# A graph kernel on one core: VectorE's comparisons read their row of numbers from PSUM instead of SBUF

## Chip, cores and metric

One NeuronCore of a Trainium2 chip. The metric is the device time of one execution in microseconds (us). The runs of the kernel before gave 4217.88, 4217.89 and 4220.7 us, median 4217.89.

## What is computed

A graph of 3125 nodes with 128 features each and 103125 edges (source, destination, one of nine types). Three relational layers, a residual with a layer norm, then one attention layer with another residual and layer norm. Cut to what matters:

```python
for l in range(3):                                  # relational layers
    X = einsum('ne,ref->rnf', out, weights[l])      # x of each node by each type
    msg = X[edge_type, src] + biases[l][edge_type]
    out = segment_sum(msg, dest); out = relu(out) if l < 2 else out
x = layernorm(x + out)
# attention over the edges: alpha = beta * cosine(x[row], x[col]), softmax over each row's edges
x = layernorm(x + segment_sum(alpha[:, None] * x[col], row))
```

The attention is done on dense score blocks; for that the kernel needs, for each pair of nodes, how many edges join them. These counts don't depend on the layers, and they are made while the layers run.

## The kernel before, in words

The edges are first sorted by the node that sums them up, into 840 tiles of 128 edges (NT), in 31 groups of 102 nodes (MB, RB). Each of the three layers then goes through the 840 tiles, in 35 turns of 24 tiles (TURNS, BODY). For each tile of a layer:

- GpSimd gathers the 128 message rows of the edges with an indirect DMA (L925, 806 of them in a layer; some of the 840 tiles share a gather). It writes them into a ring of 62 slots (`grow`) and runs ahead of the rest: before gather t it waits until tile t - 30 was used (L922 to L924).
- SP counts the gathers that have landed (`pass_on`, L824 to L827) on a semaphore that TensorE waits for (L1043).
- VectorE makes a one-hot matrix of the tile (`one_hot`, L526): 102 numbers 0 to 101 compared with each edge's row, one row of `iota_w`, 32 bits wide, in SBUF. It works eight tiles ahead (U).
- TensorE multiplies one-hot and gathered rows into PSUM bank 6 or 7, four tiles to a bank in turn (L1046, two records a tile), and VectorE adds each product to the sums in SBUF (L596). TensorE's next four tiles wait for the additions of the group before last (L1045).

The counts of edges go on beside it, five cells to twelve tiles, in layers 0 and 1 and 14 turns of layer 2 (84 turns of 10 cells). A cell is 128 edges. VectorE makes two matrices of it with comparisons of a row of 16-bit numbers, `iota_h` in SBUF (`cell_hots`, L531 with 640 elements and L532 with 510), four cells ahead. TensorE multiplies them into the five banks 0 to 4, 128 x 510 each (L1057). When a group of 102 nodes is complete, 31 times in all, ScalarE copies the five banks out (L1206) and refills them (`refill`, L1188 to L1197), and TensorE waits for it (L1056).

The order on each engine is written out by hand. VectorE's order for a tile is: wait for the four tiles' product (L586), one-hot for eight tiles later, at five of twelve tiles also the two comparisons of a cell, then the addition (`take_tiles`, L579 to L596). TensorE's order is in `use_tiles` (L1035 to L1060); at the first cell of twelve tiles it loads five numbers into registers (L1054).

Between two layers the sums are transposed (`turn_sums`, L1062, `take_turned`, L598) and multiplied by the weights of the nine types (L1080, banks 5 to 7), VectorE adds the biases (L615), and SP writes the result to memory for the gathers, for which GpSimd waits.

Bank 5 is not used while the tiles of a layer go through. L724, in the attention stage, reads PSUM and a column of scalars; L556 is an integer operation of the preparation.

Of the kernel before, what the change touches and what calls it, by code (L numbers as in the profile page):

```python
# [20 lines left out]
BF16 = mybir.dt.bfloat16  # L21
F16 = mybir.dt.float16
# [6 lines left out]
P = 128  # L29
# [16 lines left out]
def gnn_program(nc, x, src, dst, edge_type, weights, biases, beta, out):  # L46
# [92 lines left out]
    with ExitStack() as ctx:  # L139
        def sb(name, shape, dt=F32):  # L140
            return ctx.enter_context(nc.sbuf_tensor(name, shape, dt))

        def sem(name):
            return ctx.enter_context(nc.semaphore(name))
# [8 lines left out]
        diag = sb("diag", [P, 3 * P], BF16)  # L153
        zerob = sb("zerob", [P, 512], BF16)
        ones = sb("ones", [P, P])
        iota_w = sb("iota_w", [P, CG * P])
        iota_h = sb("iota_h", [P, CG * P], F16)
        x0st = sb("x0st", [P, X0 - 2, 3 * D])
        arrays = sb("arrays", [P, 9, KW])
        gix, b7, tab = (arrays[:, n, :].bitcast(I32) for n in (0, 2, 3))  # L160
# [76 lines left out]
        ps = ctx.enter_context(nc.psum_tensor("ps", [P, 8, 512], F32))  # L237


        s_edges = sem("s_edges")  # L240
        s_const = sem("s_const")
        s_pool = sem("s_pool")
# [22 lines left out]
        s_wt = sem("s_wt")  # L265
        s_wc = sem("s_wc")
        s_pt = sem("s_pt")
        s_oh = sem("s_oh")
        s_used = sem("s_used")
        s_add = sem("s_add")  # L270
# [56 lines left out]
        def _(dve):  # L327
            steps = [0]

            def step(ins, mark=None):  # L330

                steps[0] += 1
                ins.then_inc(s_d, 1)
                dve.wait_ge(s_d, steps[0])
                if mark:
                    marks[mark] = steps[0]
# [185 lines left out]
                                               op0=ALU.mult, op1=ALU.add)  # L522
            step(ins, "digits")

            def one_hot(t):
                ins = nc_.tensor_scalar(oh[:, t % U, 0:RB], iota_r, rowf[:, t % NT:t % NT + 1], None, ALU.is_equal)  # L526
                if t % SLOTS == SLOTS - 1:
                    ins.then_inc(s_oh, 1)

            def cell_hots(q):  # L530
                nc_.tensor_scalar(cl[:, q % CR, :], iota_h[:, :], key1[:, q:q + 1], None, ALU.is_equal)  # L531
                nc_.tensor_scalar(cr[:, q % CR, :], iota_h[:, 0:CW], key2[:, q:q + 1], None, ALU.is_equal).then_inc(s_co, 1)  # L532


            dve.wait_ge(s_srt, 16)
# [8 lines left out]
            dve.wait_ge(s_pt, 1)  # L544
            nc_.tensor_scalar(gix[:, 0:512], ps[:, 4, 0:512], -1.0, 0.0, ALU.add, ALU.max)
            step(nc_.tensor_scalar(gix[:, 512:GT], ps[:, 5, 0:GT - 512], -1.0, 0.0, ALU.add, ALU.max), "rows")
            for u in range(U):
                one_hot(u)

# [56 lines left out]
            for l in range(L):  # L606
                if l:
                    for n in range(HN):
                        take_turned(l, n, True)
                    for q in range(XQ):  # L610
                        b, c, u = q // XC, q % XC, q // XC % XU
                        if c == 0 and XN * (l - 1) + b // XU:
                            dve.wait_ge(s_xd[u], 16 * (XN * (l - 1) + b // XU))
                        dve.wait_ge(s_xm, XQ * (l - 1) + q + 1)
                        nc_.tensor_tensor(xst[:, u, c * G3:(c + 1) * G3], ps[:, 5 + q % XB, 0:G3],  # L615
                                          bias[:, l * RF + c * G3:l * RF + (c + 1) * G3], ALU.add).then_inc(s_xe, 1)
                        if c == 1:
                            ins = nc_.memset(hn[0:RB, b * MB * D // NB:(b + 1) * MB * D // NB], 0.0)
                    step(ins)
                full = min(TURNS, CTURNS - TURNS * l)  # L620
                for i in range(0, full):
                    take_tiles(l, i, True)
                if full < TURNS:
                    for i in range(full, TURNS):
                        take_tiles(l, i, False)
# [251 lines left out]
        @block.gpsimd  # L877
        def _(pool):
            nc_ = pool
            nc_.memset(ident[:, :], 0.0).then_inc(s_pool, 1)  # L880
            nc_.memset(ltri, 1.0).then_inc(s_pool, 1)
            nc_.memset(ones[:, :], 1.0).then_inc(s_pool, 1)
            nc_.memset(diag[:, :], 0.0).then_inc(s_pool, 1)
            nc_.iota(iota_w[:, :], pattern=[[1, CG * P]], base=0, channel_multiplier=0,
                     allow_small_or_imprecise_dtypes=True).then_inc(s_pool, 1)
            nc_.iota(iota_s, pattern=[[1, NT]], base=0, channel_multiplier=0,
                     allow_small_or_imprecise_dtypes=True).then_inc(s_pool, 1)
            nc_.iota(iota_h[:, :], pattern=[[1, CG * P]], base=0, channel_multiplier=0,
                     allow_small_or_imprecise_dtypes=True).then_inc(s_pool, 1)
            nc_.iota(number[:, :], pattern=[[P, TC]], base=0, channel_multiplier=1,  # L890
                     allow_small_or_imprecise_dtypes=True).then_inc(s_pool, 1)
            pool.wait_ge(s_pool, 8)
            nc_.affine_select(out=ident[:, :], in_=ident[:, :], compare_op=ALU.not_equal, fill=1.0, base=0,
                              pattern=[[-1, P]], channel_multiplier=1).then_inc(s_pool, 1)

            nc_.affine_select(out=ltri, in_=ltri, compare_op=ALU.is_gt, fill=0.0, base=0,
                              pattern=[[1, P]], channel_multiplier=-1).then_inc(s_pool, 1)
            pool.wait_ge(s_pool, 10)

            nc_.tensor_scalar(negi[:, :], ident[:, :], -1.0, None, ALU.mult).then_inc(s_pool, 1)  # L900
            nc_.tensor_copy(diag[:, P:2 * P], ident[:, :]).then_inc(s_pool, 1)
            pool.wait_ge(s_pool, 12)
            pool.sem_inc(s_pool, 1)

            pool.wait_ge(s_fill, 16)
            pool.wait_ge(s_d, marks["cells"])
            for t in range(CP):
                pool.indirect_dma_start(  # L908
                    out=table, out_offset=bass.IndirectOffsetOnAxis(ap=pay[:, t, 1:2], axis=0),
                    in_=pay[:, t, 0:1], in_offset=None).then_inc(s_scat, 16)  # L910

            pool.wait_ge(s_d, marks["rows"])
            for l in range(L):
                if l == 0:
                    for u in range(X0):
                        pool.wait_ge(s_x0d[u], 16 * (-(-(NB * XC - u) // X0)))
                else:
                    for u in range(XU):
                        pool.wait_ge(s_xd[u], 16 * XN * l)

                for t in range(GT):
                    last = t + SLOTS - 1 - GR + LAP  # L922
                    if t % SLOTS == 0 and t + SLOTS - 1 >= GR:
                        pool.wait_ge(s_used, NT // SLOTS * l + last // SLOTS + 1)  # L924
                    pool.indirect_dma_start(  # L925
                        out=grow[:, t % GR * D:(t % GR + 1) * D], out_offset=None, in_=xt,
                        in_offset=bass.IndirectOffsetOnAxis(ap=gix[:, t:t + 1], axis=0),
                    ).then_inc(s_g[t % GR], 16)
# [3 lines left out]
        def _(pe):  # L932
# [102 lines left out]
            def use_tiles(l, i, cells):  # L1035
                first = NT * l
                for u in range(BODY):
# [12 lines left out]
                    for q, c in PARTS[u] if cells else ():  # L1050
# [8 lines left out]
                        if c == CG - 1:  # L1059
                            mm.then_inc(s_ct, 1)  # L1060

            def turn_sums(l):  # L1062
                pe.wait_ge(s_add, NT * l + 2 * SLOTS)
                for n in range(HN):
                    if n >= XB:
                        pe.wait_ge(s_feat, HN * (l - 1) + n - XB + 1)
                    for t in range(min(SLOTS, MB - SLOTS * n)):
                        b = SLOTS * n + t
                        mm = pe.transpose(ps[:, 5 + n % XB, t * RB:(t + 1) * RB], hn[0:RB, b * D:(b + 1) * D],
                                          ident[0:RB, 0:RB])  # L1070
                    mm.then_inc(s_tn, 1)
                pe.wait_ge(s_feat, HN * l)

            for l in range(L):
                if l:
                    turn_sums(l)
                for q in range(XQ if l else 0):
                    b, c = q // XC, q % XC
                    pe.wait_ge(s_xe, XQ * (l - 1) + q + 1)
                    pe.matmul(ps[:, 5 + q % XB, 0:G3], hB[:, b * P:(b + 1) * P],  # L1080
                              wsb[:, l * R + 3 * c:l * R + 3 * c + 3, :].rearrange("p r d -> p (r d)"),
                              start=True, stop=True).then_inc(s_xm, 1)
                if l:
                    pe.wait_ge(s_xe, XB + XQ * l)
                full = min(TURNS, CTURNS - TURNS * l)
                for i in range(0, full):
                    use_tiles(l, i, True)
                if full < TURNS:
                    for i in range(full, TURNS):
                        use_tiles(l, i, False)  # L1090
# [187 lines left out]
```

## Time and profile before

| | us |
|---|---|
| median of the runs | 4217.89 |
| the profiled execution, its own time | 4214.52 |
| its span | 4212.8 |
| PE (TensorE) busy | 2935.1 (70%) |
| POOL (GpSimd) busy | 2712.7 (64%) |
| DVE (VectorE) busy | 2491.8 (59%) |
| ACT (ScalarE) busy | 820.3 (19%) |
| mean granted clock of TensorE, share of full speed | 0.818 |

The tiles of layer 0 go through from about 536 to 1611 us of the span, those of layer 1 from 1671 to 2740, those of layer 2 from 2797 to 3832; the last 380 us are the attention. An engine counts as busy while an instruction of it runs; waiting for semaphores and the issue of DMAs are not counted, but for GpSimd's indirect DMAs, whose making of descriptors shows as its busy time. Records of the profile are named by the line of the kernel. A matmul on 32-bit data shows as two records. In a timeline a row gives the start and the length in us, and in brackets how long the engine stood idle before it and what ended that; "issue" means that nothing the profile shows was waited for.

### The profile page before, as it was taken

What the parts mean: (1) busy time and instruction counts of PE and PEld (TensorE: products, weight loads), DVE (VectorE), ACT (ScalarE), POOL (GpSimd) and SP (SyncE); (2) the same over time, 40 slices, a digit from 0 to 9 for tenths busy, and PEclk for the clock granted to TensorE, in tenths of its full rate; (3) what the DMA queues carried; (4) which work ended last, traced back from release to release, by engine and by line L of the source; (5) the groups of instructions that cost most, each with busy time, mean ns of one, the idle gap of its engine ahead of it and who ended that gap; (6) DMA issues with size and microseconds to landing.
All of it is one profiled execution on the core that took longest, in us unless ns stands there. A gap on an engine that the chain in (4) does not pass through costs nothing.

```text
span 4212.8 us, 59092 instructions
## 1 busy us (share of the span) xinstructions
PE 2935.1 (70%) x14062; PEld 1899.7 (45%) x14062; DVE 2491.8 (59%) x9148; ACT 820.3 (19%) x1995; POOL 2712.7 (64%) x2738
## 2 busy tenths in 40 slices
PE   7799957666666667676666667676666444446998
PEld 4455534444444444444444434444444333334776
DVE  9988865555555456555555545565544333336999
ACT  2588701001000100100100010000001000003665
POOL 0677677777777772777777777637777777772000
PEclk9899978888888788888888888888887555556999
DMA  4100013322322334232233223243324111112554
GB/s 157 44 2 2 6 45 83 75 70 73 82 71 69 76 79 158 73 83 71 70 79 78 69 70 87 67 167 79 74 69 88 54 53 53 53 53 92 191 190 140
DMA packets 373888, 336.56 MB, mean 80 GB/s; under 512 B 262034, under 2 KB 326090, under 8 KB 373448
## 3 DMA queue, kind: packets, MB, share of 16 engines
q0 software_dynamic: 87104, 158.80, 15.2%
q1 hardware_dynamic: 83112, 113.25, 7.8%
q10 hardware_dynamic: 203360, 60.73, 5.9%
q8 instruction: 149, 2.44, 0.2%
q14 instruction: 163, 1.34, 0.1%
HBM read 225.44 MB, written 107.13 MB: 79 GB/s over the span
## 4 chain that ended last, share of the span: by engine, by line
POOL 42%; PE 26%; issue 17%; DVE 10%; DMA 3%; ACT 2%; SPq 0%; DVEq 0%; POOLq 0%; ACTq 0%
POOL region L925 42%; PE ps L1002 9%; PE ps L1057 5%; PE ps L1046 4%; DMA region<-x_of_type,arrays 3%; PE ps L1109 2%; PE ps L1080 2%; PE ps L1137 2%; DVE region L596 1%; DVE region L373 1%; DVE region L707 1%; DVE region L531 1%; DVE arrays L407 1%; DVE arrays L418 1%; ACT ps L1195 1%
## 5 line engine op out<-in xcount | busy, mean ns | idle before, releaser
L925 POOL DMA_INDIRECT region<-x_of_type,arrays x2418 | 2411.9, 997 | 902.2 <-issue 716.2
L1057 PE MATMUL ps<-region 128*128 128x510 f16 x4200 | 1466.2, 439 | 536.6 <-issue 341.1
L526 DVE TENSOR_SCALAR oh<-iota_w,arrays 128x102 f32<-128x102 f32 x2528 | 719.4, 285 | 1619.4 <-PE ps L1046 1601.5
L1046 PE MATMUL ps<-region,oh 128*102 x5040 | 1155.3, 334 | 640.3 <-SPq L827 511.3
L1046 PEld LDWEIGHTS ps<-region,oh 128*102 128x102 f32 x5040 | 981.3, 215 | 1220.0 <-issue 958.0
L1057 PEld LDWEIGHTS ps<-region 128*128 128x128 f16 x4200 | 445.3, 109 | 650.9 <-issue 600.7
L596 DVE TENSOR_TENSOR region<-region,ps 102x128 f32 x2520 | 712.7, 283 | 3.2 <-issue 3.1
L1206 ACT COPY region<-ps 128x510 f32<-128x510 f32 x155 | 89.8, 580 | 2447.0 <-PE ps L1057 2446.6
L908 POOL DMA_INDIRECT scattered_edges<-region x304 | 296.3, 975 | 208.3 <-DVE shiftcol L437 110.6
L1002 PE MATMUL ps<-region 128*128 128x420 f16 x2016 | 361.2, 341 | 23.0 <-ACT region L1176 23.0
L531 DVE TENSOR_SCALAR region<-iota_h,arrays 128x640 f16<-128x640 f16 x844 | 331.3, 393 | 0.0
L1176 ACT ACTIVATE region<-region 128x128 f16<-128x128 f16 x1008 | 310.0, 389 | 69.2 <-DVE region L507 68.9
L532 DVE TENSOR_SCALAR region<-iota_h,arrays 128x510 f16<-128x510 f16 x844 | 296.7, 352 | 0.0
L1002 PEld LDWEIGHTS ps<-region 128*128 128x128 f16 x2016 | 195.5, 97 | 189.3 <-ACT region L1176 24.1
L508 DVE TENSOR_SCALAR region<-region 128x840 f16<-128x840 f16 x504 | 262.5, 521 | 0.0
L1137 PEld LDWEIGHTS ps<-nodes,region 128*128 128x128 f32 (+1 forms) x1250 | 163.8, 191 | 53.9 <-DVE region L707 28.5
L1137 PE MATMUL ps<-nodes,region 128*128 128x129 f32 (+1 forms) x1250 | 181.3, 282 | 7.2 <-DVE region L707 7.0
L1109 PE MATMUL ps<-hB,region 128*128 128x384 f32 (+1 forms) x450 | 170.8, 461 | 0.0
L507 DVE TENSOR_SCALAR region<-region 128x128 f16<-128x128 f16 x504 | 128.0, 254 | 35.5 <-PE ps L1002 35.3
L1241 ACT COPY region<-ps 128x384 f32<-128x384 f32 (+1 forms) x225 | 101.5, 452 | 93.8 <-PE ps L1112 91.2
L1250 ACT ACTIVATE region<-region 128x384 f32<-128x384 f32 (+1 forms) x225 | 112.0, 498 | 34.4 <-DVE region L698 31.9
L679 DVE TENSOR_TENSOR region<-region 128x384 f32<-128x384 f32 (+1 forms) x216 | 112.0, 519 | 10.8 <-ACT region L1241 9.3
(215 smaller groups left out, 1432.5 us busy)
## 6 DMA issues: line engine op xcount, KB each, us to landing
edge_counts<-region ACTq DMA_DIRECT2D x155, 255.0 KB
region<-x_of_type,arrays POOLq DMA_INDIRECT x2418, 2.5
arrays<-edge_counts SPq DMA_DIRECT2D x40, 960.0 KB, 4.8
x_of_type<-region SPq DMA_DIRECT2D x50, 576.0 KB, 2.7
edge_absent<-region ACTq DMA_DIRECT2D x155, 127.5 KB
region<-edge_absent SPq DMA_DIRECT2D x40, 480.0 KB, 3.8
x_of_type<-x0st SPq DMA_DIRECT2D x51, 192.0 KB, 1.8
scattered_edges<-region POOLq DMA_INDIRECT x304
```

The costliest lines, as they stand in the source:

```text
L508: nc_.tensor_scalar(oh_s[:, k, :], iota_s, c, None, ALU.is_equal).then_inc(s_cell, 1)
L526: ins = nc_.tensor_scalar(oh[:, t % U, 0:RB], iota_r, rowf[:, t % NT:t % NT + 1], None, ALU.is_equal)
L531: nc_.tensor_scalar(cl[:, q % CR, :], iota_h[:, :], key1[:, q:q + 1], None, ALU.is_equal)
L532: nc_.tensor_scalar(cr[:, q % CR, :], iota_h[:, 0:CW], key2[:, q:q + 1], None, ALU.is_equal).then_inc(s_co, 1)
L596: nc_.tensor_tensor(h, h, ps[0:RB, 6 + n % 2, t * D:(t + 1) * D], ALU.add).then_inc(s_add, 1)
L908: pool.indirect_dma_start(out=table, out_offset=bass.IndirectOffsetOnAxis(ap=pay[:, t, 1:2], axis=0), in_=pay[:, t, 0:1], in_offset=None). ...
L925: pool.indirect_dma_start(out=grow[:, t % GR * D:(t % GR + 1) * D], out_offset=None, in_=xt, in_offset=bass.IndirectOffsetOnAxis(ap=gix[:, ...
L1002: mm = pe.matmul(ps[:, 2 * d + n, 0:HW], oh_q[:, k, d, :], oh_s[:, k, n * HW:(n + 1) * HW], start=False, stop=False, skip_group_check=True)
L1046: mm = pe.matmul(ps[0:RB, 6 + n % 2, t * D:(t + 1) * D], oh[:, u % U, 0:RB], grow[:, bass.ds(at[u % PAIRS], D)], start=True, stop=True)
L1057: mm = pe.matmul(ps[:, c, 0:CW], cl[:, q % CR, c * P:(c + 1) * P], cr[:, q % CR, :], start=False, stop=False, skip_group_check=True)
L1137: mm = pe.matmul(ps[0:w, 4 + c % 2, t * VW:(t + 1) * VW], ring[:, b % RING, t * P:t * P + w], nodes[:, j, :], start=False, stop=(j == NB - ...
L1176: ins = act.activation(oh_q[:, k, d, :], hot_q[:, k, :], ACT.Copy, scale=cols[:, 4 * t + 2 + d:4 * t + 3 + d])
```

## The change

VectorE's two kinds of comparisons no longer read their row of numbers from SBUF but from PSUM bank 5, where columns 0 to 101 hold the 32-bit row (`lane_r`) and the following 320 words the 640 16-bit numbers (`lane_h`). The 32-bit row is copied there by VectorE (`load_lanes`), the 16-bit one put there by five transposes on TensorE (`turn_steps`) of a new tile `steps_down`, which holds the numbers down the partitions. Both are done once a layer, since the steps between layers use bank 5: in layer 0 before the first one-hots, in layers 1 and 2 after the last product of x and weights. The comparisons' outputs stay in SBUF.

```diff
-        iota_w = sb("iota_w", [P, CG * P])
-        iota_h = sb("iota_h", [P, CG * P], F16)
+        iota_w = sb("iota_w", [P, RB])
+        steps_down = sb("steps_down", [P, CG * P], F16)
+        lane_r = ps[:, 5, 0:RB]
+        lane_h = ps[:, 5, RB:RB + CG * P // 2].bitcast(F16)
...
+            def load_lanes(l):
+                dve.wait_ge(s_ln, 1 + l)
+                step(nc_.tensor_copy(lane_r, iota_r))
+
             def one_hot(t):
-                ins = nc_.tensor_scalar(oh[:, t % U, 0:RB], iota_r, rowf[:, t % NT:t % NT + 1], None, ALU.is_equal)
+                ins = nc_.tensor_scalar(oh[:, t % U, 0:RB], lane_r, rowf[:, t % NT:t % NT + 1], None, ALU.is_equal)
...
             def cell_hots(q):
-                nc_.tensor_scalar(cl[:, q % CR, :], iota_h[:, :], key1[:, q:q + 1], None, ALU.is_equal)
-                nc_.tensor_scalar(cr[:, q % CR, :], iota_h[:, 0:CW], key2[:, q:q + 1], None, ALU.is_equal).then_inc(s_co, 1)
+                nc_.tensor_scalar(cl[:, q % CR, :], lane_h, key1[:, q:q + 1], None, ALU.is_equal)
+                nc_.tensor_scalar(cr[:, q % CR, :], lane_h[:, 0:CW], key2[:, q:q + 1], None, ALU.is_equal).then_inc(s_co, 1)
...
             step(nc_.tensor_scalar(gix[:, 512:GT], ps[:, 5, 0:GT - 512], -1.0, 0.0, ALU.add, ALU.max), "rows")
+            load_lanes(0)
             for u in range(U):
                 one_hot(u)
...
                     step(ins)
+                    load_lanes(l)
                 full = min(TURNS, CTURNS - TURNS * l)
...
-            nc_.iota(iota_w[:, :], pattern=[[1, CG * P]], base=0, channel_multiplier=0,
+            nc_.iota(iota_w[:, :], pattern=[[1, RB]], base=0, channel_multiplier=0,
...
-            nc_.iota(iota_h[:, :], pattern=[[1, CG * P]], base=0, channel_multiplier=0,
+            nc_.iota(steps_down[:, :].rearrange("p (b m) -> p b m", m=P), pattern=[[P, CG], [0, P]], base=0, channel_multiplier=1,
...
+            def turn_steps():
+                for b in range(CG):
+                    mm = pe.transpose(ps[:, 5, RB + b * P // 2:RB + (b + 1) * P // 2].bitcast(BF16),
+                                      steps_down[:, b * P:(b + 1) * P].bitcast(BF16), diag[:, P:2 * P])
+                mm.then_inc(s_ln, 1)
+
+            turn_steps()
...
                 if l:
                     pe.wait_ge(s_xe, XB + XQ * l)
+                    turn_steps()
```

## Rows read from the trace of the kernel before

**Rows 1.** Chain that ended last: shares by line

```profile
POOL region L925 42%; PE ps L1002 9%; PE ps L1057 5%; PE ps L1046 4%; DMA region<-x_of_type,arrays 3%; PE ps L1109 2%; PE ps L1080 2%; PE ps L1137 2%; DVE region L596 1%; DVE region L373 1%; DVE region L707 1%; DVE region L531 1%; DVE arrays L407 1%; DVE arrays L418 1%; ACT ps L1195 1%
```

**Rows 2.** Windows of L925 alone: stretch, its length, POOL busy (count), clock, DMA, GB/s

```profile
536.00:1600.30 1064.30, 818.50 (x806) 0.83 0.30 73
1671.00:2728.50 1057.50, 811.42 (x806) 0.84 0.31 75
2797.00:3228.00 431.00, 330.73 (x330) 0.83 0.31 74
3228.00:3826.00 598.00, 451.03 (x477) 0.50 0.20 56
```

**Rows 3.** L925: durations min/median/max; then a wait of POOL in the layers

```profile
L925 POOL DMA_INDIRECT region<-x_of_type,arrays x2418: 938/944/1552, 535.9 to 3823.1; - x186
...
POOL region L925 <- PE ps L1046: 19.8, 65, 0.3
```

**Rows 4.** Timeline of POOL and VectorE (start, length), 1759 to 1763 us

```profile
1759.59 0.94 POOL L925 DMA_INDIRECT region<-x_of_type,arrays  x1 [0.30 <-issue]
...
1762.10 1.32 POOL L925 DMA_INDIRECT region<-x_of_type,arrays  x1 [0.30 <-issue]
...
1761.96 0.38 DVE L531 TENSOR_SCALAR region<-iota_h,arrays 128x640 f16<-128x640 f16 x1
1762.25 0.35 DVE L532 TENSOR_SCALAR region<-iota_h,arrays 128x510 f16<-128x510 f16 x1
```

**Rows 5.** Groups of instructions: count, busy us, mean ns, idle before them

```profile
L526 DVE TENSOR_SCALAR oh<-iota_w,arrays 128x102 f32<-128x102 f32 x2528 | 719.4, 285 | 1619.4 <-PE ps L1046 1601.5 <-issue 4.1
L596 DVE TENSOR_TENSOR region<-region,ps 102x128 f32 x2520 | 712.7, 283 | 3.2 <-issue 3.1
L531 DVE TENSOR_SCALAR region<-iota_h,arrays 128x640 f16<-128x640 f16 x844 | 331.3, 393 | 0.0
L532 DVE TENSOR_SCALAR region<-iota_h,arrays 128x510 f16<-128x510 f16 x844 | 296.7, 352 | 0.0
L602 DVE TENSOR_SCALAR hB<-ps 128x408 f32<-128x408 f32 (+1 forms) x16 | 8.2, 564 | 1.6 <-PE ps L1069 1.3
L556 DVE SCALAR_TENSOR_TENSOR arrays<-arrays 128x840 int32<-128x840 int32 x1 | 1.0, 1034 | 0.0
```

**Rows 6.** Timeline of VectorE: runs of one instruction without a wait

```profile
535.71 1.58 DVE L526 TENSOR_SCALAR oh<-iota_w,arrays 128x102 f32<-128x102 f32 x8
...
3936.47 0.86 DVE L724 SCALAR_TENSOR_TENSOR wsb<-ps,rden,nodes 128x128 f32<-128x128 f32 x3
```

**Rows 7.** Timeline of TensorE and VectorE over twelve tiles, 653 to 667 us

```profile
653.45 0.46 PE L1046 MATMUL ps<-region,oh 128*102 x2
666.80 0.46 PE L1046 MATMUL ps<-region,oh 128*102 x2
...
660.84 0.27 DVE L526 TENSOR_SCALAR oh<-iota_w,arrays 128x102 f32<-128x102 f32 x1 [5.38 <-PE ps L1046]
666.27 0.28 DVE L596 TENSOR_TENSOR region<-region,ps 102x128 f32 x1
```

**Rows 8.** Timeline of TensorE around two refills of the count banks

```profile
1769.17 0.46 PE L1046 MATMUL ps<-region,oh 128*102 x2 [2.69 <-SPq L827]
...
1783.30 0.58 PE L1057 MATMUL ps<-region 128*128 128x510 f16 x1 [6.16 <-ACT ps L1195]
...
1804.07 0.46 PE L1046 MATMUL ps<-region,oh 128*102 x2 [0.57 <-DVE region L596]
...
2012.11 0.75 PE L1046 MATMUL ps<-region,oh 128*102 x2 [3.19 <-SPq L827]
...
2042.66 0.46 PE L1046 MATMUL ps<-region,oh 128*102 x2
```

**Rows 9.** Waits of TensorE, 1677 to 2728 us, then 3228 to 3826 us

```profile
PE ps L1046 <- SPq L827: 82.2, 39, 10.6
...
PE ps L1046 <- SPq L827: 316.8, 107, 4.6
```

More of the change, by code:

```diff
@@ L237, in gnn_program @@
         ps = ctx.enter_context(nc.psum_tensor("ps", [P, 8, 512], F32))
+        lane_r = ps[:, 5, 0:RB]
+        lane_h = ps[:, 5, RB:RB + CG * P // 2].bitcast(F16)
+        assert RB + CG * P // 2 <= 512
         s_edges = sem("s_edges")
@@ L267, in gnn_program @@
         s_pt = sem("s_pt")
+        s_ln = sem("s_ln")
         s_oh = sem("s_oh")
```

## The prediction, made before the changed kernel ran

> **What bounds the kernel now.** I read the chain of waits first. One line, the gather of a tile (L925, an indirect DMA that GpSimd issues), holds 42% of the 4212.8 us of the span, four times the next [rows 1]. The windows of that line alone then give the pace of each layer: some 806 gathers in 1064, 1058 and 1029 us (431 and 598 for the two parts of layer 2), 1.02, 1.01, 1.00 and 0.95 us of GpSimd apiece [rows 2]. The fastest part is the one without edge counts (3228 to 3826 us). The same line's durations have a median of 944 ns but reach 1552, and inside the layers it waits for TensorE only 19.8 us, never more than 0.3 [rows 3]. So GpSimd runs without a stop at 0.944 + 0.30 = 1.248 us a gather, and what it has above that is its own lengthening: 2411.7 - 2418 x 0.944 = 129 us, of which 57.6 in layer 0, 50.6 in layer 1, 19.2 in the part of layer 2 with counts and 0.7 in the part without [rows 2, 3].
>
> The timeline shows what the long gathers lie beside: the one at 1762.10 takes 1.32 us while the two comparisons for the counts run (1761.96 to 1762.60), the one at 1759.59 takes 0.94 with VectorE idle [rows 4]. Where only one-hots and additions run beside it, 477 gathers are longer by 0.7 us in all [rows 2]: so it is the 16-bit comparisons, back to back, that cost GpSimd. The Trainium skill ("SBUF — State Buffer", Who interferes with whom) says that VectorE in a mode with two SBUF ports locks GpSimd out for the whole instruction, whichever instruction it is. By that the one-hots would cost as well, which these rows don't show, and the gain would still be the 129 us that are there.
>
> The second thing to see is that TensorE and VectorE have little to spare while counts are made. TensorE stands idle behind SP's count of landed tiles for 82 us of 1051 in layer 1, but for 317 of 598 where no counts are made [rows 9]. Once it is late, it shows its own pace: twelve tiles and five count cells from 653.45 to 666.80 us, 13.35 us, with no wait for a gather in between. GpSimd needs 12 x 806/840 x 1.30 = 15.0 us for them now, and 14.4 us at 1.248.
>
> **The change part by part.** *GpSimd's lengthening* can go altogether: -129 us, if nothing else is late. That is the whole of the possible gain, and the floor.
>
> *VectorE's three reads.* Per element, a two-source operation takes (1034 - 283)/(840 - 128) = 1.055 ns [rows 5]. The one-hot (102 elements, 32 bits) starts every (1.58 - 0.27)/7 = 0.187 us [rows 6], which is 0.054 for the elements at half that rate and 0.133 fixed. A 32-bit PSUM source goes at the full 1.055: the 128 elements of L724, with a scalar column like the one-hot's, start every (0.86 - 0.34)/2 = 0.26 us, again 0.135 + 0.125 fixed [rows 6]. So the one-hot gains 0.054 us. For the 16-bit rows the trace has no PSUM read. From SBUF they differ by 393 - 352 = 41 ns for 130 elements [rows 5], near a quarter of 1.055 each: 16 bits run twice as fast as 32 from the same place. The lower bound is no change (the same four at a time), the upper one 1.055 ns an element as in L602's reads of PSUM (564 ns for 408) [rows 5]: +0.51 us for the 640 and +0.40 for the 510. I take the halving that SBUF shows, so 0.53 ns an element: +0.17 and +0.13, together +0.30 us a cell. VectorE's sum is 2528 x 0.054 + 844 x 0.30 = 390 us more work in a part where it idles 1619 us [rows 5], so it does not become the bound by its total; what counts is its place in the chain.
>
> The skill speaks against this: "VectorE: DVE Perf Modes", The TRN2 errata, gives a PSUM source 120 fixed cycles where an SBUF source has 58. By it each of the reads would cost some 65 ns more, and the sum below would end near 4370. The rows don't bear it out: 0.125 us fixed from PSUM, 0.133 from SBUF [rows 6].
>
> *The chain that takes over.* Between 653.45 and 666.80 [rows 7] TensorE takes 7.4 us from its first tile to the release of VectorE (660.84; a register load lies in it), VectorE then works through eight tiles and four cells without a stop until 666.55, and 0.25 us later TensorE begins the next twelve: its tiles wait for the additions of the group before last (L1045), since two PSUM banks alternate. So VectorE's time for eight tiles and four cells, 5.7 us, lies on the path in full. It grows by 8 x 0.054 + 4 x 0.30 = 1.63 us. What it wins back where it stood behind GpSimd is 285 - 270 ns on a one-hot and 13 on a cell's first comparison [rows 5, 7], 0.2 us. Twelve tiles then take 13.3 + 1.4 = 14.7 us. This is above GpSimd's 14.4.
>
> To it come the refills. After each of the 31 blocks of edges ScalarE copies out five banks and TensorE waits 6.2 us for it. Two runs of 24 tiles around a refill took 1804.07 - 1769.17 = 34.9 and 2042.66 - 2012.11 = 30.6 us, with 2.7 and 3.2 us of waiting for SP in them [rows 8]. Where TensorE is late anyway that waiting goes, at least in part; I take 31.6, and 2.2 more for VectorE (half of it hides behind ScalarE): 33.8. A block has 84 x 24/31 = 65 tiles, 5.42 times twelve, and a layer 12.9 blocks. A block takes 33.8 + 3.42 x 14.7 = 84.1 us against 1064/12.9 = 82.5 now, or 20.6 us more for each of layers 0 and 1. In layer 2 the lateness grows over 5.5 blocks to some 30 us, is worked off where no counts are made (317 us idle there), and GpSimd's 20 us are won. GpSimd may run about 30 gathers (37 us) ahead, more towards the end, so it doesn't stop for that.
>
> *Small parts.* In layer 0 the transposes stand behind TensorE's six zeroing matmuls, and VectorE's first one-hots wait for them, 4 us that its chain keeps. In layers 1 and 2 the transposes and the copy are hidden by the last write of x and the first gathers, over 6 us; without that cover they would cost some 2 us each. No DMA and no queue is moved past. GpSimd's two rows of numbers at the start are made while inputs load: nothing.
>
> *The sum:* 4214.5 (the profiled execution's own time) + 41 - 20 + 4 = 4239.5; that execution is 3.4 us under the median of the runs, so **4243 us**.
>
> **The rivals.**
> *A, GpSimd stays the bound:* TensorE and VectorE keep up and the lengthening is simply gone. For it: every layer's pace is GpSimd's today [rows 2, 3]. Against: it needs twelve tiles in 12.9 us late in a block, less than the 13.35 they take today. 4214.5 - 129 = 4085.5, so 4089, up to 4150 when it is met in part. Chance 0.15.
> *B, 16 bits from PSUM come one at a time:* +0.6 us a cell more, twelve tiles 17.1 us, a block 94.7, 157 us a layer and 25 in layer 2: 4562. The trace has no such read; the halving speaks against it. Chance 0.06.
> *C, the lengthening has another cause* and stays: +41 + 4, 4263. Against it: 0.7 us in the part without cells. Chance 0.08.
> *D, a read from PSUM lets no neighbour overlap:* an overlap of 0.27 - 0.187 = 0.08 us lost on 16 instructions, 1.3 us, twelve tiles 16.0: 4426. L724 speaks against it [rows 6]. Chance 0.05. (The skill's larger fixed part, above, would show in this way.)
> *The forecast's case* has 0.66. Each 0.1 us on twelve tiles is 12.7 us of the whole; 14.1 to 15.2 us gives 4165 to 4310.
>
> **The numbers.** 0.2%, what a measurement can tell here, is 8.4 us: 4209.5 to 4226.3 counts as the same. Twelve tiles at 14.45 to 14.57 would land there, 0.13. Faster: A and the lower part of the forecast's case (under 14.45), 0.15 + 0.23 = 0.38. Slower: the rest of it and B, C, D, 0.49. The range 4105 to 4345 leaves out the lower part of A (0.08), B and D: 0.19.
>
> **What would show it.** Right: L925's maximum near its median of 944 ns; the cell comparisons at about 0.55 and 0.48 us, the one-hot near 0.32; GpSimd waiting for TensorE towards the end of layers 0 and 1; TensorE's wait for SP near nothing while counts are made. Wrong: cell comparisons near 0.9 us (B); twelve late tiles below 14 us, that is VectorE's part of the chain growing by less than it should; L925 still at a mean of 997 ns (C); starts of reads in a run further apart than 0.26 us (D).

## The result and the profile after

The changed kernel takes 4169.16 us (median of 4 runs, 4163.54 to 4171.98), the kernel before 4219.3 beside it (4217.88 to 4224.06): a ratio of 0.9878, 95% interval 0.986 to 0.9895. It is faster by 1.2%, where 4243 us, a slowing of 0.6%, was forecast; the time lies within the range given.

The profile of the changed kernel, span 4170.2 us: the chain that ended last, its shares by engine and then by line. L936 is the gather, L1057 and L1068 TensorE's tiles and cells, L535 the one-hot, L540 and L541 a cell's two comparisons, L606 the addition, L838 SP's count of landed tiles.

```profile
PE 35%; DVE 31%; POOL 14%; issue 13%; ACT 4%; DMA 2%; DVEq 1%; SPq 0%; POOLq 0%; ACTq 0%
POOL region L936 14%; PE ps L1068 11%; PE ps L1013 9%; DVE region L540 8%; DVE region L606 7%; PE ps L1057 7%; DVE region L541 6%; DVE oh L535 3%; PE ps L1129 2%; PE ps L1099 2%; PE ps L1157 2%; DMA region<-x_of_type,arrays 2%; ACT ps L1215 2%; ACT region L1226 2%; DVE region L378 1%
```

Beside [rows 1] one sees the bound change hands: the gather had 42%, now TensorE's and VectorE's six lines of tiles and cells hold 42% together (11 + 8 + 7 + 7 + 6 + 3) and the gather 14%. The groups of instructions of the same kernel (count, busy us, mean ns, idle before):

```profile
L936 POOL DMA_INDIRECT region<-x_of_type,arrays x2418 | 2283.9, 945 | 990.3 <-issue 717.1 <-DMA x_of_type<-region 227.3 <-DVE arrays L555 27.0
L535 DVE TENSOR_SCALAR oh<-ps,arrays 128x102 f32<-128x102 f32 x2528 | 803.2, 318 | 1275.4 <-PE ps L1057 1250.3 <-issue 7.0
L606 DVE TENSOR_TENSOR region<-region,ps 102x128 f32 x2520 | 695.3, 276 | 3.7 <-issue 3.6
L540 DVE TENSOR_SCALAR region<-ps,arrays 128x640 f16<-128x640 f16 x844 | 455.7, 540 | 0.0
L541 DVE TENSOR_SCALAR region<-ps,arrays 128x510 f16<-128x510 f16 x844 | 398.7, 472 | 0.0
```

Against [rows 3, 5]: the gathers' mean is down from 997 to 945 ns, their busy time from 2411.9 to 2283.9 us. The three comparisons are longer by 33, 147 and 120 ns. GpSimd's freed time comes back as waiting: at the two changes of layer together it waits 227.3 us for the new x, 140.3 before. It is done with a layer when TensorE and VectorE are not. The windows of L936 alone (stretch, length, POOL busy and count, clock, DMA, GB/s) show it, to be read beside [rows 2]:

```profile
535.00:1544.00 1009.00, 763.05 (x806) 0.83 0.31 75
1658.00:2665.00 1007.00, 760.48 (x806) 0.84 0.32 77
```

The ends of the layers, first tile of TensorE and last addition of VectorE, in the timelines of the changed kernel:

```profile
542.24 0.75 PE L1057 MATMUL ps<-region,oh 128*102 x2 [5.57 <-SPq L838]
1598.82 0.28 DVE L606 TENSOR_TENSOR region<-region,ps 102x128 f32 x1
1665.24 0.53 PE L1057 MATMUL ps<-region,oh 128*102 x1 [9.60 <-SPq L838]
2715.38 0.27 DVE L606 TENSOR_TENSOR region<-region,ps 102x128 f32 x1
2783.38 0.75 PE L1057 MATMUL ps<-region,oh 128*102 x2 [9.59 <-SPq L838]
3790.21 0.29 DVE L606 TENSOR_TENSOR region<-region,ps 102x128 f32 x1
```

and of the kernel before:

```profile
543.54 0.75 PE L1046 MATMUL ps<-region,oh 128*102 x2 [6.52 <-SPq L827]
1611.02 0.29 DVE L596 TENSOR_TENSOR region<-region,ps 102x128 f32 x1
1677.38 0.75 PE L1046 MATMUL ps<-region,oh 128*102 x2 [10.64 <-SPq L827]
2739.36 0.29 DVE L596 TENSOR_TENSOR region<-region,ps 102x128 f32 x1
2803.57 0.75 PE L1046 MATMUL ps<-region,oh 128*102 x2 [10.66 <-SPq L827]
3831.49 0.29 DVE L596 TENSOR_TENSOR region<-region,ps 102x128 f32 x1
```

From the first tile to the last addition the layers took 1067.5, 1062.0 and 1027.9 us before (start to start) and take 1056.6, 1050.1 and 1006.8 now: 10.9, 11.9 and 21.1 less. That is 43.9 us, and the two spans differ by 42.6: the layers are the whole of it. From layer 0's last addition to layer 1's first tile it is 66.4 us in both. From its first gather to its last GpSimd needs 1008 and 1006 us for layers 0 and 1, so over 40 us of each are the new chain's. Twelve late tiles, with TensorE's row at their start, VectorE's first one-hot behind it, a cell, the last addition before the release and the next start:

```profile
659.51 0.46 PE L1057 MATMUL ps<-region,oh 128*102 x2 [0.81 <-DVE region L606]
666.45 0.32 DVE L535 TENSOR_SCALAR oh<-ps,arrays 128x102 f32<-128x102 f32 x1 [4.62 <-PE ps L1057]
666.69 0.54 DVE L540 TENSOR_SCALAR region<-ps,arrays 128x640 f16<-128x640 f16 x1
667.15 0.47 DVE L541 TENSOR_SCALAR region<-ps,arrays 128x510 f16<-128x510 f16 x1
667.54 0.27 DVE L606 TENSOR_TENSOR region<-region,ps 102x128 f32 x1
673.29 0.28 DVE L606 TENSOR_TENSOR region<-region,ps 102x128 f32 x1
673.82 0.46 PE L1057 MATMUL ps<-region,oh 128*102 x2 [0.79 <-DVE region L606]
```

It is the pattern of [rows 7]: TensorE until 666.45, VectorE without a stop until 673.57, 0.25 us, the next twelve. A cell's starts are 0.46 and 0.39 us apart here (666.69, 667.15, 667.54). TensorE's waits in the stretch of layer 1, 1658 to 2716 us, are for the additions now (72.3 us, 30.3 before) and hardly for SP (18.4 us, of which 9.6 at the layer's start; 82.2 in [rows 9]):

```profile
PE ps L1057 <- DVE region L606: 72.3, 94, 1.2
...
PE ps L1057 <- SPq L838: 18.4, 11, 9.6
```

### The profile page after: what moved, and what is told of

It is laid out like the page before. It is cut to its first block, busy times and chain, and to the rows that moved or that the text cites. A ratio compares the mean times of both kernels' runs of the same rounds, so it can differ in the third digit from the quotient of the medians.

```text
span 4170.2 us, 59126 instructions
## 1 busy us (share of the span) xinstructions
PE 2947.4 (71%) x14075; PEld 1900.5 (46%) x14077; DVE 2787.4 (67%) x9151; ACT 820.1 (20%) x1995; POOL 2583.0 (62%) x2738
## 4 chain that ended last, share of the span: by engine, by line
PE 35%; DVE 31%; POOL 14%; issue 13%; ACT 4%; DMA 2%; DVEq 1%; SPq 0%; POOLq 0%; ACTq 0%
POOL region L936 14%; PE ps L1068 11%; PE ps L1013 9%; DVE region L540 8%; DVE region L606 7%; PE ps L1057 7%; DVE region L541 6%; DVE oh L535 3%; PE ps L1129 2%; PE ps L1099 2%; PE ps L1157 2%; DMA region<-x_of_type,arrays 2%; ACT ps L1215 2%; ACT region L1226 2%; DVE region L378 1%
## 5 line engine op out<-in xcount | busy, mean ns | idle before, releaser
L936 POOL DMA_INDIRECT region<-x_of_type,arrays x2418 | 2283.9, 945 | 990.3 <-issue 717.1
L1068 PE MATMUL ps<-region 128*128 128x510 f16 x4200 | 1469.0, 440 | 554.1 <-issue 295.5
L535 DVE TENSOR_SCALAR oh<-ps,arrays 128x102 f32<-128x102 f32 x2528 | 803.2, 318 | 1275.4 <-PE ps L1057 1250.3
L1057 PE MATMUL ps<-region,oh 128*102 x5040 | 1157.9, 335 | 565.0 <-SPq L838 348.4
L1057 PEld LDWEIGHTS ps<-region,oh 128*102 128x102 f32 x5040 | 978.3, 214 | 1152.7 <-issue 892.7
L1068 PEld LDWEIGHTS ps<-region 128*128 128x128 f16 x4200 | 448.3, 110 | 668.6 <-issue 616.1
L606 DVE TENSOR_TENSOR region<-region,ps 102x128 f32 x2520 | 695.3, 276 | 3.7 <-issue 3.6
L540 DVE TENSOR_SCALAR region<-ps,arrays 128x640 f16<-128x640 f16 x844 | 455.7, 540 | 0.0
L541 DVE TENSOR_SCALAR region<-ps,arrays 128x510 f16<-128x510 f16 x844 | 398.7, 472 | 0.0
L690 DVE TENSOR_TENSOR region<-region 128x384 f32<-128x384 f32 (+1 forms) x216 | 111.8, 518 | 10.6 <-ACT region L1261 9.1
L1270 ACT ACTIVATE region<-region 128x384 f32<-128x384 f32 (+1 forms) x225 | 112.0, 498 | 34.4 <-DVE region L709 31.9
```

Source lines behind the costliest of these rows:

```text
L535: ins = nc_.tensor_scalar(oh[:, t % U, 0:RB], lane_r, rowf[:, t % NT:t % NT + 1], None, ALU.is_equal)
L540: nc_.tensor_scalar(cl[:, q % CR, :], lane_h, key1[:, q:q + 1], None, ALU.is_equal)
L541: nc_.tensor_scalar(cr[:, q % CR, :], lane_h[:, 0:CW], key2[:, q:q + 1], None, ALU.is_equal).then_inc(s_co, 1)
L606: nc_.tensor_tensor(h, h, ps[0:RB, 6 + n % 2, t * D:(t + 1) * D], ALU.add).then_inc(s_add, 1)
L936: pool.indirect_dma_start(out=grow[:, t % GR * D:(t % GR + 1) * D], out_offset=None, in_=xt, in_offset=bass.IndirectOffsetOnAxis(ap=gix[:, ...
L1057: mm = pe.matmul(ps[0:RB, 6 + n % 2, t * D:(t + 1) * D], oh[:, u % U, 0:RB], grow[:, bass.ds(at[u % PAIRS], D)], start=True, stop=True)
```

## The experiments

### Parts of the change

The three kernels between before and after, from the changed one; the setting up of bank 5 stays in all. Each experiment ran beside the kernel before on the same chip, and its ratio is to that: 4209.61 us beside the first four runs, 4210.51 beside the repetitions further down. *Cells only* reads the one-hots' row from SBUF:

```diff
-    ins = nc_.tensor_scalar(oh[:, t % U, 0:RB], lane_r, ...)
+    ins = nc_.tensor_scalar(oh[:, t % U, 0:RB], iota_r, ...)
```

> The changed kernel, but the 32-bit one-hots read SBUF again (0.27 us in place of 0.318). Theory (VectorE's time for eight tiles and four cells lies in full on the path of every late twelve tiles): 8 x 0.05 = 0.4 us less on twelve, 14.0 to 13.6 us, times 4.9 a block and 12.9 blocks in two layers: some 50 us less, 4120 us. The gathers stay at 0.944 us, since the one-hots cost GpSimd little in the part without counts. Rival 1 (VectorE's part isn't what makes the late twelve long, TensorE's own is): 4165 to 4170. Rival 2 (a one-hot that reads SBUF lengthens gathers beside a cell's comparisons): mean of the gathers over 0.96 us and less gain.

Measured 4129.86 us, 0.9812 (0.9794 to 0.983), the gathers' mean 946 ns. By the ratios (0.9812 and 0.9878) it is better than the change itself by 0.66%, or 28 us, where some 50 were expected: the one-hots bring next to nothing for GpSimd, and their longer time sits on the chain. Over its 108 late twelves (counted as further down) VectorE's part is 6.9 us where the changed kernel has 7.2, 0.25 us less and not 0.4.

*One-hots only* has both cell comparisons read `iota_h` from SBUF (an iota as before):

```diff
-    nc_.tensor_scalar(cl[:, q % CR, :], lane_h, ...)
-    nc_.tensor_scalar(cr[:, q % CR, :], lane_h[:, 0:CW], ...)
+    nc_.tensor_scalar(cl[:, q % CR, :], iota_h[:, :], ...)
+    nc_.tensor_scalar(cr[:, q % CR, :], iota_h[:, 0:CW], ...)
```

> The changed kernel, but both 16-bit comparisons read SBUF again. Theory: they are what lengthens the gathers, so the mean of the gathers is 0.98 us or more and GpSimd sets the pace again; the chain has 8 x 0.05 us more than before and would be at 13.3 to 13.7. 4190 to 4215 us. Rival (the long gathers come from the run of three such instructions with the one-hot in it): mean of the gathers under 0.96 us and a time of 4110 to 4140.

Measured 4184.04 us, 0.9941 (0.9923 to 0.9959), a little under what was expected. *The 510 only* has the one-hots and the 640 elements in SBUF and the 510 alone in PSUM:

```diff
-    ins = nc_.tensor_scalar(oh[:, t % U, 0:RB], lane_r, ...)
+    ins = nc_.tensor_scalar(oh[:, t % U, 0:RB], iota_r, ...)
-    nc_.tensor_scalar(cl[:, q % CR, :], lane_h, ...)
+    nc_.tensor_scalar(cl[:, q % CR, :], iota_h[:, :], ...)
```

> Only the second 16-bit comparison (510 elements) reads PSUM, the other and the one-hots SBUF. Theory: the long gathers of before lie beside the run of one-hot and both comparisons, about 0.9 us of two-port reads; with the last one out of it the run is 0.5 us and the gathers' excess falls from 129 us to under 30. VectorE's eight tiles and four cells take 5.63 + 4 x 0.12 = 6.1 us, a late twelve 13.3 us: 4095 to 4125 us. Rival (each two-port instruction lengthens gathers by its own share): excess of 60 us or more, mean of the gathers 0.97, and 4140 to 4170.

Measured 4144.73 us, 0.9852 (0.9835 to 0.9868): slower than the theory had it, in the range of its rival. The gathers kept 53 us of their lengthening, where the theory gave under 30 and the rival 60 or more. The gather's group in the three, in this order:

```profile
L936 POOL DMA_INDIRECT region<-x_of_type,arrays x2418 | 2286.7, 946 | 943.7 <-issue 718.0 <-DMA x_of_type<-region 180.7 <-DVE arrays L555 27.0
```
```profile
L939 POOL DMA_INDIRECT region<-x_of_type,arrays x2418 | 2382.0, 985 | 903.2 <-issue 721.4 <-DMA x_of_type<-region 140.1 <-DVE arrays L556 27.0
```
```profile
L939 POOL DMA_INDIRECT region<-x_of_type,arrays x2418 | 2335.7, 966 | 905.8 <-issue 718.9 <-DMA x_of_type<-region 143.0 <-DVE arrays L556 26.8
```

Above 2418 x 0.944 = 2282.6 us that is 4 us, 99 us and 53 us, beside 129 before and 1 after. In SBUF are then, one behind the other: a one-hot; the two comparisons; a one-hot and one comparison; all three (before). A one-hot alone and the two comparisons alone make 103 us, all three in a row 129. So the prices don't simply add; that it is how long VectorE's reads from SBUF follow each other without a break, the last run of the next section shows.

### Cells behind the additions

VectorE makes the comparisons of a group's cells after its four additions, so that TensorE's bank is released first. (At the end of a layer TensorE also waits for the last cells before bank 5 is used otherwise.)

```diff
                     for q, c in PARTS[u]:
                         if cells and c == 1:
-                            dve.wait_ge(s_ct, ...)
-                            cell_hots(...)
+                            later.append(q)
                     dve.wait_ge(s_add, i * BODY + (first + u + 2 * SLOTS))
...
+                    if t == SLOTS - 1:
+                        for q in later:
+                            dve.wait_ge(s_ct, ...)
+                            cell_hots(...)
...
             def turn_sums(l):
+                pe.wait_ge(s_co, min(CTURNS, TURNS * l) * CB + CR - 1)
```

> The changed kernel; VectorE makes the cells of a group of four tiles after the group's four additions, not between them. The same instructions, the same lengths. Theory (TensorE's twelve wait for the additions of the group before last, and all that VectorE does ahead of them is on the path): the cells of the second group leave the path, 2 x 0.86 us less, 12.3 us a late twelve, under GpSimd's 14.4, so GpSimd sets the pace: 4080 to 4100 us. Rival (the total of VectorE's work or TensorE's own pace is what takes 14.0 us): within 10 us of 4169.

Measured 4089.76 us, 0.9717 (0.9701 to 0.9734). With the same instructions and the same lengths as in the changed kernel (318, 543 and 474 ns in the profile of its repetition), what the chain had cost is gone. A second time:

> The changed kernel with the cells behind the four additions, a second time, beside the other two on one chip: 4085 to 4095 us.

4089.86 us, 0.9716 (0.9703 to 0.9729). The window of its gathers in layer 1 and TensorE's wait for SP over the whole span:

```profile
1616.90:2622.80 1005.90, 760.49 (x806) 0.85 0.35 79
```
```profile
PE ps L1060 <- SPq L841: 442.7, 187, 9.7
```

TensorE waits for gathers again (348.4 us after the change, 442.7 here), at the two changes of layer GpSimd waits 143.8 us together, near the 140.3 of before, and the gather's line has 32% of the chain that ended last where the changed kernel had 14%: GpSimd is the bound, now at 1.248 us a gather. That is rival A's time of 4089, reached by another order and not by the change alone.

With the one-hots from SBUF as well:

> Cells read PSUM, one-hots SBUF, cells behind the four additions, again for the same reason. Theory (GpSimd at 1.249 us a gather sets the pace everywhere): 4084 to 4092 us. Rival (the chain still sets it behind refills): 4070 to 4080.

4094.3 us, 0.9723 (0.971 to 0.9736), 2 us above the theory's range and 4 us more than with them in PSUM, within the intervals of both. Where GpSimd is the bound, a shorter one-hot gains nothing.

Then the same order in the kernel before, all three rows of numbers in SBUF. It asks whether the order alone brings the gain. (What the expectation says of the first run's chip is taken up below.)

> The kernel before with the cells behind the four additions, again, since the chip of the first run landed its gathers late (5270 us for the kernel before). Theory (the lengthened gathers set the pace): 4190 to 4212 us, gathers at a mean near 0.99 us. Rival (the order is the gain by itself): 4090 to 4130 us.

Measured 4356.82 us, 1.0337 (1.0323 to 1.0351): both expectations missed, and slower by 3.4%. Its gather's group, and POOL and VectorE where two cells follow each other:

```profile
L928 POOL DMA_INDIRECT region<-x_of_type,arrays x2418 | 2562.2, 1060 | 899.6 <-issue 721.4 <-DMA x_of_type<-region 137.7 <-DVE arrays L546 25.9
```
```profile
1761.47 0.38 DVE L531 TENSOR_SCALAR region<-iota_h,arrays 128x640 f16<-128x640 f16 x1
1761.77 0.35 DVE L532 TENSOR_SCALAR region<-iota_h,arrays 128x510 f16<-128x510 f16 x1
1761.92 1.75 POOL L928 DMA_INDIRECT region<-x_of_type,arrays  x1 [0.30 <-issue]
...
1762.03 0.38 DVE L531 TENSOR_SCALAR region<-iota_h,arrays 128x640 f16<-128x640 f16 x1
...
1762.33 0.35 DVE L532 TENSOR_SCALAR region<-iota_h,arrays 128x510 f16<-128x510 f16 x1
...
1762.59 0.27 DVE L526 TENSOR_SCALAR oh<-iota_w,arrays 128x102 f32<-128x102 f32 x1
```

The gather starts at 1761.92. The four comparisons and the one-hot that follows them without a break end at 1762.86, 0.94 us later; the gather is longer by 1.75 - 0.94 = 0.81. The lengthening sums to 2562.2 - 2282.6 = 280 us instead of 129, for the same instructions in longer runs. So the order needs the rows in PSUM: with them it brings 0.9878 to 0.9716, alone it is harmful (1.0337).

These two kernels had run before, on a chip on which the kernel before itself took 5270.08 us:

> The kernel before (all comparisons read SBUF), with the cells behind the four additions as in the run of the changed kernel. Theory (GpSimd's lengthened gathers set its pace, 1.30 us each): shorter late twelves win next to nothing, 4195 to 4212 us, gathers at a mean near 0.99 us. Rival (the order is the gain by itself and PSUM has no part in it): 4090 to 4130 us.

> Cells read PSUM, one-hots SBUF, cells behind the four additions. Theory: GpSimd sets the pace in all layers, as in the changed kernel with that order (4090 us), so 8 x 0.05 us less of VectorE's time wins next to nothing: 4084 to 4092 us. Rival (the chain still sets it behind refills): 4070 to 4080.

Measured 5191.44 us, 0.9842 (0.9821 to 0.9863), and 5237.7 us, 0.9944 (0.992 to 0.9968). The expectations of the repetitions blame gathers that land late there; that is not what held these runs up: TensorE waited for SP 38.0 us in the first, 685.2 in its repetition. What both profiles show is VectorE standing idle before a one-hot for 1273.9 us in 204 stretches and 1306.5 us in 208 that nothing on the core ended ("remote" in the profile), and the repetitions have none of these. The order alone came out 1.6% faster there and 3.4% slower in the repetition; since something else set the time, the first runs test neither expectation, and what held VectorE up stays open.

### TensorE and VectorE without GpSimd

Every second gather is left out in the kernel before and in the changed one (the ring is zeroed once, SP doesn't count the missing ones), so that messages are missing from the sums, and GpSimd hardly bounds a layer. This shows the chain's own pace.

```diff
+            step(nc_.memset(grow, 0.0))
...
-                    sp.wait_ge(s_g[t % GR], ...)
+                    if t % 2 == 0:
+                        sp.wait_ge(s_g[t % GR], ...)
...
+                    if t % 2:
+                        continue
```

> The kernel before with every second gather left out (those tiles use rows of another gather or zeros), so that GpSimd can't set the pace and every twelve tiles is late: the chain of TensorE and VectorE by itself, with the old comparisons. Open is why the late twelves of the changed kernel take 14.0 us and not 14.7: TensorE's part is 6.6 us there against 7.1 in the 22 late ones of before. Theory 1 (those 22 were no fair sample, most of them right behind a refill; TensorE's part is 6.6 us whenever lateness lasts): a twelve takes 12.8 us, layers 0 and 1 985 to 1000 us. Theory 2 (TensorE's part is shorter in the changed kernel because VectorE is slower, TensorE standing idle elsewhere instead): 7.1 us here too, a twelve 13.25 us, layers 1005 to 1020 us.

> The changed kernel with every second gather left out in the same way. Its layers 0 and 1 are late throughout already, so both theories expect them where they are, 1050 to 1060 us, and late twelves at 14.0 us. If GpSimd's gathers still had a hand in them, they would be shorter. Layer 2 falls below 1007 us, which GpSimd sets now.

They ran once each on that same chip, so their whole times (4104.73 and 4353.51 us) are compared with nothing; but in layer 1 TensorE waited for SP once in before, at the start, and 5.4 us in all behind the start in after. Before takes 954.7 and 969.3 us for layers 0 and 1, shorter than both theories; after takes 1061.6 and 1069.7, somewhat over the expected 1050 to 1060, and 808.1 for layer 2, under 1007 as expected. Each has the stall of this chip near the start of a layer, before a one-hot of VectorE (17.5 and 27.9 us in before, 13.5 and 27.5 in after), so it nearly drops out of the difference: VectorE's longer comparisons cost the chain 100 to 107 us a layer. Windows of twelve tiles each in layer 1, in before:

```profile
2113.15:2125.91 12.76, 10.25 (x50) 6.66 (x49) 7.49 (x34) 0.00 (x0) 6.22 (x7) 0.83 0.46 107
2125.91:2137.60 11.69, 8.64 (x49) 5.58 (x50) 8.13 (x36) 0.00 (x0) 6.74 (x7) 1.00 0.43 81
2137.60:2148.23 10.63, 8.64 (x49) 5.59 (x50) 7.31 (x32) 0.00 (x0) 6.11 (x6) 1.00 0.47 75
2148.23:2161.31 13.08, 10.32 (x49) 6.46 (x50) 8.12 (x36) 0.00 (x0) 6.47 (x7) 0.87 0.13 31
```

and in after (the columns, as above, are the stretch, its length, PE, PEld, DVE, ACT and POOL busy with counts, granted clock, DMA, GB/s):

```profile
2233.78:2249.01 15.23, 11.57 (x50) 7.04 (x49) 9.29 (x34) 0.00 (x0) 6.26 (x7) 0.71 0.44 107
2249.01:2263.38 14.37, 10.32 (x49) 6.47 (x50) 9.56 (x35) 0.00 (x0) 5.68 (x6) 0.88 0.37 67
2263.38:2276.78 13.40, 10.32 (x50) 6.45 (x50) 9.57 (x35) 0.00 (x0) 5.67 (x6) 0.87 0.23 45
```

A twelve counts as late where it holds no refill and the next one begins within 0.4 us of the addition that releases it. Over the late twelves of layers 0 and 1 the mean is 12.03 us in before (103 of them, without the one that holds the stall of 27.9 us) and 13.68 in after (111). The pace varies with the granted clock: 10.6 to 11.7 us at 1.00, 12.8 to 13.1 at 0.83 to 0.87. (1.00 is the level of 2.4 GHz; below it a part of the stretch was at 1.2.)

## Why the prediction was wrong

- **GpSimd's lengthening goes**: right, in size and place. 129 us became 1; L936's median is 944 ns as before. The gathers that are still long (up to 1432 ns) lie in the first 20 us of layer 0, beside other instructions on SBUF. (The pause between two gathers is 716.2/2350 = 0.305 us; with it the prediction's 0.944 + 0.30 comes to 1.249, and the trace has 1.248.)
- **What causes it**: half right. The comparisons beside a gather cost it, as *one-hots only* and *cells only* show (rival C is out), but it is not a matter of 16 bits. Eight one-hots without a break, in *cells only*, from SBUF:

```profile
538.76 1.56 DVE L535 TENSOR_SCALAR oh<-iota_w,arrays 128x102 f32<-128x102 f32 x8
539.55 1.39 POOL L936 DMA_INDIRECT region<-x_of_type,arrays  x1 [0.30 <-issue]
```

and in the changed kernel, from PSUM, with the gather as far into the run:

```profile
537.07 1.94 DVE L535 TENSOR_SCALAR oh<-ps,arrays 128x102 f32<-128x102 f32 x8
537.86 0.94 POOL L936 DMA_INDIRECT region<-x_of_type,arrays  x1 [0.31 <-issue]
```

1.39 against 0.94 us: 32-bit one-hots from SBUF lengthen a gather too, if they stand in a row. Single one-hots cost next to nothing (4 us over 2528 in *cells only*), and I had taken that for a sign that only 16 bits cost. The traces show the rule when all gathers beside an unbroken run of SBUF reads are sorted by their start. In the kernel before, those that start 0.1 to 0.2 us into a run of three (55 of them) have 0.67 us of it before them and are longer by 0.53 in the median; 0.5 to 0.6 us into it (125), 0.26 and 0.11. With four or five in a row, 0.2 to 0.3 us into the run (32), it is 1.06 and 0.91. So the lengthening is about what is left of the run, less some 0.15 us, and of a single one-hot of 0.27 us next to nothing is left to cost. Gathers that start within the first 0.1 us of a run of three (34) are not longer in the median, with 0.78 us before them. The section of the Trainium skill that the prediction set aside ("SBUF — State Buffer", Who interferes with whom) says that whoever issues first gets the shared pair of ports for the whole instruction and that the other blocks. The trace agrees for gathers that start well inside a run, if the unbroken run is taken for the instruction. It doesn't for some of those that start up to 0.5 us ahead of a run and are lengthened all the same (80 at 0.3 to 0.4 us ahead, median 0.36). Nothing in the prediction's sum hung on it.
- **VectorE's reads**: right. 16 bits from PSUM come two at a time: 540 and 472 ns, starts 0.46 and 0.39 us apart where SBUF had 0.30 and 0.26 (a cell +0.29, forecast +0.30). The one-hots' starts in a run are (1.94 - 0.32)/7 = 0.231 us apart from PSUM, 0.187 from SBUF: +0.044, forecast +0.054. Rivals B and D are out.
- **The sum of 4370 that the prediction set aside**: rightly, but for another reason than it gave. The table of the Trainium skill ("VectorE: DVE Perf Modes", The TRN2 errata) gives VectorE 120 fixed cycles of 0.96 GHz from PSUM and 58 from SBUF. With one 32-bit or two 16-bit elements a cycle its figure for PSUM comes to (120 + 102)/0.96 = 231 ns for the one-hot and to 458 and 391 ns for the two comparisons, estimates from that table. The traces agree: starts 0.231, 0.46 and 0.39 us apart. Its figure for SBUF does not fit: (58 + 51)/0.96 = 114 ns, again an estimate from the table, where the one-hots start 0.187 us apart. So PSUM costs what the table says and SBUF costs more, and the 65 ns between the two, on which the 4370 rested, are not there.
- **The chain of TensorE and VectorE takes over**: right, it bounds layers 0 and 1 (the chain that ended last is TensorE's for 35% and VectorE's for 31% of the span, 26% and 10% before, and GpSimd waits at the layers' ends). GpSimd as the bound (rival A) is out for this kernel.
- **Its pace, 14.7 us on twelve tiles: this is the step that failed.** Of a layer of 1056.6 us, 12.9 blocks of 81.9 us, two runs of twelve around a refill take 34 us (687.31 to 721.68 is 34.4; forecast 33.8), which leaves (81.9 - 34) / 3.42 = 14.0 us. Counted one by one, 110 twelves in layers 0 and 1 of after are late, with a mean of 13.8 us; split as the prediction did, their means are 6.4 us for TensorE's part where 7.4 were forecast, and 7.2 for VectorE's (forecast 5.7 + 1.4 = 7.1). VectorE's growth was right; TensorE's part was not. It had been read from one stretch, 653.45 to 660.84. The windows of the kernel before for that stretch and the one behind it:

```profile
653.45:660.84 7.39, 4.50 (x16) 2.75 (x17) 2.01 (x10) 0.00 (x0) 5.68 (x6) 0.77 0.50 105
660.84:666.55 5.71, 5.64 (x34) 3.70 (x32) 5.58 (x25) 0.00 (x0) 4.37 (x5) 1.00 0.29 72
```

The granted clock was 0.77 in it. The 26 late twelves of before's layers 0 and 1 have a mean of 12.6 us, not 13.3, and of 6.4 for TensorE's part; 18 of them are shorter than the one that was read. With half the gathers the mean is 12.0. The spread is nearly all TensorE's part and goes with the clock: of the 110 late twelves of after, 19 had a granted 1.00 and took 4.4 us for TensorE's part, 61 had 0.86 to 0.90 and took 6.6, 29 had less than 0.80 and took 7.5, while VectorE's part was 7.2 in all three groups. In before's 26 it is 4.0 (6 of them), 6.9 (14) and 7.4 (6). The forecast took 7.4 for every twelve.
- **The sum with 14.0 in place of 14.7**: a block takes 33.8 + 3.42 x 14.0 = 81.7 against 82.5, 10 us less for a layer (measured 10.9 and 11.9, forecast 20.6 more). Layer 2: -20 forecast, -21.1 measured. Start of layer 0: +4 forecast, none seen (the first tile comes 1.3 us earlier). 4214.5 - 20 - 20 = 4174.5, and the profiled execution took about that: its span is 4170.2. One number of 0.7 us, counted 88 times, turned the sign. (The prediction prices 0.1 us on twelve tiles at 12.7 us, which counts the twelves at refills too; its own sum has 8.8 for TensorE's part.)
- **Why so little came of so much**: the time is the larger of two terms, and the change moves both. GpSimd goes from 1064 and 1057 us a layer to 1008 and 1006; the chain goes from 955 and 969 (half the gathers, with 18 and 28 us of stall in them) to 1057 and 1050. The chain took GpSimd's place, so that of GpSimd's 56 and 51 us a layer 11 and 12 were left. With the cells behind the additions it doesn't.

## What to carry to other kernels

Where VectorE's instructions on SBUF lengthen what GpSimd issues, look at how long they run without a break, and take one source out of SBUF where the runs are longest; leave short ones, which cost next to nothing, alone (*cells only*: a ratio of 0.981 against 0.988). If the edited engine is next in line, have it release what the next engine waits for first, and then do its slower work (4090 us), but try such an order only together with the other edit (alone 4357, since it makes the runs longer). And take a pace for a forecast from the mean of all stretches of its kind, with the clock of each beside it.

## What the runs showed of the hardware that was not expected

- The lengthening of a gather grows faster than the time of the comparisons beside it: 4 us in all with single one-hots, 53 with a one-hot and a comparison, 99 with the two comparisons, 129 with all three, 280 where 197 runs are four comparisons and a one-hot and 139 more have four in a row. A gather loses about what is left of the run when it starts, less some 0.15 us, so doubling a run does more than double its price. What sets these 0.15 us, and why a gather that starts just ahead of a run can be lengthened too, was not tried.
- With half the gathers TensorE's part is shorter where VectorE is faster: the late twelves differ by 1.65 us, of which VectorE's eight tiles are 1.35 (5.54 and 6.89 from the first one-hot to the eighth addition) and TensorE's part 0.32 (5.94 and 6.26), of which 1.8 us stood at the lower clock in the one and 2.9 in the other. With all gathers TensorE's part is 6.35 us before and 6.42 after, with 3.1 and 3.2 us at the lower clock, so this is not what the change did. What sets that share was not tried.
